# A GNN layer and a 64-expert FFN on one core: shared products deferred, a weight slot loaded earlier, another shape for the overflow turn

## The reference

```
x = x + relu(segment_sum(w * (layernorm(x) @ W)[dst], by src) + bias)      # 16384 edges
xt = layernorm(x);  scores = sigmoid(xt @ Wg.T + bg);  top 2 of 64, weights normed
nx = layernorm(xt)
y = sum over the 2 experts e of  weight * (silu(nx' @ W1[e] + b1) * (nx' @ W3[e] + b3)) @ W2[e] + b2
z = (silu(nxs @ Ws1 + bs1) * (nxs @ Ws3 + bs3)) @ Ws2 + bs2                 # shared expert, hidden 32
x = x + y + z
```

## Time and profile before

| | us |
|---|---|
| median of 3 runs | 459.57 |
| the profiled execution, its own time | 458.82 |
| its span, first to last instruction | 457.1 |
| TensorE busy | 391.7 (86%) |
| VectorE busy | 207.7 (45%) |
| ScalarE busy | 166.1 (36%) |
| GpSimd busy | 154.9 (34%) |
| mean granted TensorE clock | 0.932 of full speed |

### The profile page before, as it was taken

The page is one execution under the profiler, slowest core; times in us unless marked ns, Lnnn a source line. Parts: engine busy times, 40 slices in busy tenths (PEclk is TensorE's granted clock), DMA queues, the critical chain, the costliest instruction groups (busy, mean ns, idle before and its releaser), DMA issues.

```text
span 457.1 us, 6545 instructions
## 1 busy us (share of the span) xinstructions
PE 391.7 (86%) x1811; PEld 202.3 (44%) x1812; DVE 207.7 (45%) x685; ACT 166.1 (36%) x414; POOL 154.9 (34%) x262
## 2 busy tenths in 40 slices
PE   2699999999999987999999999986988979888600
PEld 1586767656565553344344443433434433343100
DVE  5889888216666586532333233313113123222036
ACT  9859999223223220233233323331213231131200
POOL 2575553014654657232333223323113122110000
PEclk9989999999999995899999999999889898898855
DMA  4999600100004545499999999999999999996068
GB/s 113 328 383 408 276 0 0 42 25 24 24 25 122 222 156 197 144 389 408 404 408 407 405 408 409 407 406 408 407 406 409 406 405 404 403 405 271 20 250 303
DMA packets 41779, 126.11 MB, mean 276 GB/s; under 512 B 7953, under 2 KB 8529, under 8 KB 41618
## 3 DMA queue, kind: packets, MB, share of 16 engines
q1 hardware_dynamic: 35954, 117.29, 66.3%
q0 software_dynamic: 5792, 8.43, 5.3%
HBM read 121.22 MB, written 13.39 MB: 294 GB/s over the span
## 4 chain that ended last, share of the span: by engine, by line
PE 81%; issue 5%; DMA 5%; DVE 3%; SPq 3%; POOL 1%; ACT 1%; ACTq 0%; DVEq 0%; POOLq 0%
PE bank L1295 29%; PE bank L1312 13%; PE bank L1168 12%; PE bank L1129 6%; PE bank L1136 6%; PE bank L1304 5%; PE bank L1288 4%; DMA w<-totals 2%; DMA X<-in_x_dram 2%; PE bank L1156 2%; PE bank L1187 1%; PE bank L1236 1%; PE bank L1177 1%; PE bank L1117 1%; SPq L398 1%
## 5 line engine op out<-in xcount | busy, mean ns | idle before, releaser
L1031 DVE SCALAR_TENSOR_TENSOR osl<-bank,b13T,osl 128x64 f32<-128x64 f32 x132 | 28.4, 277 | 171.5 <-ACT osl L675 171.5
L1295 PE MATMUL bank<-w,xhT 128*64 128x512 f32 x368 | 91.9, 645 | 14.7 <-issue 14.5
L668 ACT COPY xh<-bank 128x512 f32<-128x512 f32 x33 | 19.3, 585 | 149.0 <-PE bank L1295 149.0
L1168 PE MATMUL bank<-HW,AT 128*128 128x512 f32 x128 | 58.2, 592 | 0.0
L1295 PEld LDWEIGHTS bank<-w,xhT 128*64 128x64 f32 x368 | 28.6, 147 | 61.5 <-issue 60.1
L545 POOL DMA_INDIRECT totals<-osl,A x17 | 17.0, 1000 | 91.5 <-PE bank L1288 72.1
L1312 PE MATMUL bank<-w,osl 128*64 128x512 f32 x184 | 45.0, 608 | 3.2 <-DVE osl L1031 3.2
L545 POOL DMA_INDIRECT totals<-GW,A x16 | 16.0, 999 | 87.2 <-PE bank L1288 71.6
L587 ACT ACTIVATE osl<-iota,eT 128x128 f32<-128x128 f32 x128 | 39.0, 389 | 6.1 <-PE bank L1129 6.1
L541 POOL DMA_INDIRECT A<-nx_rows,A x33 | 34.4, 1041 | 10.5 <-issue 10.5
L1168 PEld LDWEIGHTS bank<-HW,AT 128*128 128x128 f32 x128 | 22.9, 191 | 21.0 <-issue 21.0
(11 more groups left out here) (208 smaller groups left out, 543.2 us busy)
## 6 DMA issues: line engine op xcount, KB each, us to landing
w<-in_L_ffn_W_dram SPq DMA_DIRECT2D x66, 1024.0 KB
A<-in_L_ffn_W_dram SPq DMA_DIRECT2D x15, 1024.0 KB
HW<-in_L_ffn_W_dram SPq DMA_DIRECT2D x10, 1024.0 KB
AT<-in_L_ffn_W_dram SPq DMA_DIRECT2D x5, 1024.0 KB
w<-totals SPq DMA_DIRECT2D x8, 512.0 KB, 7.5
w<-in_L_ffn_W_dram SPq DMA_DIRECT2D x6, 512.0 KB
X<-in_x_dram SPq DMA_DIRECT2D x4, 512.0 KB, 7.2
out_dram<-X SPq DMA_DIRECT2D x8, 256.0 KB, 5.7
```

Of the source, the lines that this page charges most:

```text
L1031: ins = v.scalar_tensor_tensor(hT[b][:, m, CAP * h:CAP * h + CAP], bank[4][:, (HC + m) * P + CAP * h:(HC + m) * P + CAP * h + CAP], b13T[: ...
L1168: ins = t.matmul(bank[4 + s % 2][:, :], AT[:, s % 2, k, :], HW[:, k, :], start=(k == 0), stop=(k == NB - 1))
L1295: ins = t.matmul(bank[2 + b][CAP * h:CAP * h + CAP, :], xe[b][:, c, CAP * h:CAP * h + CAP], up_w[v][:, h, :, c, :], start=(c == 0), stop=( ...
```

## The change

1. The list is read into the tile `xg[3]` instead of `M`, so its read does not wait for the last block of X. On SP the loads of slot 5 now stand at s = 6, ahead of the list's read and of the last `nx_rows` store.
2. `shared(5..7)` are taken out of the stretch before turn 0 and put into turns 20, 22 and 24 (`late_turn`), with their `add_shared`. `add_shared(0..2)` come before the overflow count on VectorE, `add_shared(3..4)` in turn 0, the last `transpose_stack` in turn 2. GpSimd does `stacked(7)` after the first gather instead of before it.
3. `keep_busy(bank, n)`: n transposes of the identity into a bank that is not read: 24 before turn 0's rows, 8 before the overflow turn's `up`, 14 before its `down`.
4. An overflow turn takes one expert and up to 128 more tokens (`steps` at 64, 192, ...), with `over_up`, `over_down`, `over_silu` and `over_product` on 128 rows at once: half as many, twice as wide instructions, and half the weights. `LIST` is 2 N, so `slots` and the memset and store that fill it are twice as large. The number of overflow turns is now the number of such experts (chunks), not half of it.

```diff
-LIST = N
+LIST = 2 * N
...
-        Lflat = M[0:PAIRS, 0, 0:2, :].rearrange("j a n -> j (a n)")
+        Lflat = xg[XG - 1][0:PAIRS, 0:2 * CAP * REC]
...
+        LATE = 5
+        late_turn = [PAIRS - 12, PAIRS - 10, PAIRS - 8]
...
                 if s == NB - 2:
-                    for i in range(2):
-                        sp.wait_ge(rec_out[i], 32 * DRAM_BLOCKS // 2)
-                    sp.wait_ge(x1_ready, NB)
-                    sp.dma_start(L, lists[:, :, 0:CAP * REC]).then_inc(list_in, 16)
-                if s == NB - 1:
                     sp.wait_ge(out_ps, NB)
                     load_up(RING // 2 + 1, RING // 2 + 1)
                     load_down(RING // 2 + 1, RING // 2 + 1)
+                    for i in range(2):
+                        sp.wait_ge(rec_out[i], 32 * DRAM_BLOCKS // 2)
+                    sp.dma_start(L, lists[:, :, 0:CAP * REC]).then_inc(list_in, 16)
...
             for j in range(AHEAD):
                 gather(TOK[:, j:j + 1], j)
+                if j == 0:
+                    stacked(NB - 1)
...
-            shared(5)
-            shared(6)
-            transpose_stack(NB - 1)
-            shared(7)
+            def keep_busy(spare_bank, n):
+                for i in range(n):
+                    t.transpose(spare_bank[:, (i % DC) * P:(i % DC + 1) * P], ident[:, :], ident[:, :])
...
+            def over_up(b):
+                for c in range(DC):
+                    ins = t.matmul(bank[2 + b][:, :], xe[b][:, c, :], up_w[OS][:, 0, :, c, :], start=(c == 0), stop=(c == DC - 1))
+                ins.then_inc(h_ps, 1)
...
+            pe.wait_ge(vs_ready, NB)
+            keep_busy(bank[0], 24)
             pe.wait_ge(xg_in[0], 16)
             turn_rows(0, 0)
             pe.wait_ge(extra_ready, 1)
-            pe.wait_ge(z_added, NB)
+            pe.wait_ge(z_added, 3)
...
+                if j in late_turn:
+                    shared(LATE + late_turn.index(j))
                 pe.wait_ge(xe_ready, j + 1)
+                if j == 0:
+                    pe.wait_ge(stackT_ready, NB - 1)
+                if j == PAIRS:
+                    pe.wait_ge(z_added, NB)
+                    keep_busy(bank[5], 8)
...
+                if j < PAIRS:
+                    up(j % 2, j % SLOTS)
+                else:
+                    over_up(j % 2)
...
+            keep_busy(bank[5], 14)
             down_of(PAIRS)
```

More of the change, by code:

```diff
@@ L27 @@
 OVER = 2 * N // CAP
+STEPS = N // P
 REC = 2
@@ L525, in stacked @@
                 g.tensor_tensor(stack[i][:, 0:64], weighted, other, ALU.add).then_inc(stack_ready, 1)
-            for s in range(NB + 1):
-                if s < NB:
-                    deviations(s)
+            for s in range(NB):
+                deviations(s)
                 if s > DRAM_BLOCKS:
@@ L682, in result, with over_silu @@
                 a.copy(ysb[i], bank[6 + b][:, :]).then_inc(y_ready, 1)
[L684 to L686 removed]
+            def over_silu(j, b, t):
+                e = act.value_load(over_expert[0:1, ds(t, 1)], min_val=0, max_val=EXPERTS - 1)
+                act.wait_ge(hT_ps, j + 1)
+                for m in range(HC):
+                    ins = a.activation(sl[b][:, m, :], bank[4][:, m * P:m * P + P], ACT.Silu, bias=b13T[:, 0, m, ds(e, 1)])
+                ins.then_inc(sl_ready, 1)
             for j in range(PAIRS + 1):
@@ L971, in _ @@
             stack_out(NB - 2)
+            for b in range(3):
+                add_shared(b)
             dve.wait_ge(count_ps, 1)
-            mark(v.tensor_scalar(steps[:, 0:CHUNKS - 1], iota[0:64, 1:CHUNKS], float(CAP), None, ALU.mult))
+            mark(v.tensor_scalar(steps[:, 0:STEPS], iota[0:64, 0:STEPS], float(P), float(CAP), ALU.mult, ALU.add))
             mark(v.tensor_scalar(expert_at, spare[0:64, :], float(CHUNKS), 1.0 - EXPERTS * CHUNKS - N * CHUNKS, ALU.mult, ALU.add))
             link(v.tensor_copy(count, list_bank[0:64, 128:129]))
[L976 to L981, removed]
+            link(v.tensor_scalar(passed[:, 0:STEPS], steps[:, 0:STEPS], count, None, ALU.is_lt))
+            v.tensor_reduce(extra, passed[:, 0:STEPS], AX, ALU.add).then_inc(extra_ready, 1)
             def over_table():
@@ L1035, in product, with over_product @@
                 ins.then_inc(hT_ready, 1)
+            def over_product(j, b, e):
+                dve.wait_ge(sl_ready, j + 1)
+                for m in range(HC):
+                    ins = v.scalar_tensor_tensor(hT[b][:, m, :], bank[4][:, (HC + m) * P:(HC + m) * P + P], b13T[:, 1, m, ds(e, 1)], sl[b][:, m, :],
+                                                 ALU.add, ALU.mult)
+                ins.then_inc(hT_ready, 1)
             def over_at_expert(t):
-                return [dve.value_load(over_expert[0:1, ds(2 * t + h, 1)], min_val=0, max_val=EXPERTS - 1) for h in range(2)]
+                return dve.value_load(over_expert[0:1, ds(t, 1)], min_val=0, max_val=EXPERTS - 1)
             rows(0, 0)
@@ L1049, in _ @@
                     rows(j + 1, (j + 1) % 2)
+                if j == 0:
+                    for b in range(3, LATE):
+                        add_shared(b)
+                    dve.wait_ge(stack_ready, NB)
+                if j == 2:
+                    stack_out(NB - 1, bank[5])
+                if j in late_turn:
+                    add_shared(LATE + late_turn.index(j))
                 if j == PAIRS // 2:
@@ L1297, in up, with over_down @@
                 ins.then_inc(h_ps, 1)
+            def over_up(b):
+                for c in range(DC):
+                    ins = t.matmul(bank[2 + b][:, :], xe[b][:, c, :], up_w[OS][:, 0, :, c, :], start=(c == 0), stop=(c == DC - 1))
+                ins.then_inc(h_ps, 1)
+            def over_down(j, b):
+                pe.wait_ge(hT_ready, j + 1)
+                for m in range(HC):
+                    ins = t.matmul(bank[6 + b][:, :], hT[b][:, m, :], down_w[OS][:, 0, m, :], start=(m == 0), stop=(m == HC - 1))
+                ins.then_inc(y_ps, 1)
             def turn_hidden(j, b):
```

110 lines of the change are left out of this document (59 added, 51 removed).

## The result

The changed kernel takes 455.86 us (median of 7 runs, 454.87 to 457.12); the kernel before, run beside it, 459.0 us (7 runs, 457.39 to 460.67). The ratio is 0.9934, with a 95% interval of 0.9911 to 0.9958: faster by 3.1 us, where 7.5 us were forecast. A second measurement of the same two kernels (label a2_change_again) gave 455.83 against 458.38, ratio 0.9942 [0.9916, 0.9968]. The profiled execution took 455.27 us; its span is 453.5 us (before: 457.1), its mean granted clock 0.959 (before: 0.932).

A forecast was written before the change was run, and what follows sets the result against it. Weight stream bounds it from about 300 us, starting when `up(0)` ends. Gain 7.5 us: 2.0 start, 1.1 wait, 1.8 clock in `up(32)`, about 1.1 silu and product, 1.5 clock in `down(32)`; forecast 452.1 us, range 449.0 to 457.0.

The forecast's parts named there:

- the start term: Start of the weight stream: `up(0)` ends 2.0 us earlier, between a loss of 1 and a gain of 5.
- the list lands near 170.7: List's read behind slot 5's weights on SP: lands near 170.7 us, where it landed at 166.3 before.
- 4 us, if its record scatters are slowed too: Upper bound on how late `list_ready` comes, before turn 0; the lower bound was nothing, if the list passes the weights.
- `list_ready` at 174.9: Before the first gather: `rank(7)` 1.9 us late at about 172.5, so `list_ready` at 174.9 instead of 172.75.
- The end term: Last turn: 1.1 us wait, 1.8 clock in `up(32)`, about 1.1 silu and product, 1.5 clock in `down(32)`.
- the plateau from the 17th slice on: Weight stream in the profile before: DMA share 9 tenths, 403 to 409 GB/s from about 188 us.
- Hidden parts: Late shared products in turns 20, 22, 24 and the doubled `slots` fill cost nothing; uncovered, 0.9 us each and 1.3 us.
- A: Rival: identity transposes before turn 0 and in the last turn do not hold the clock; gain 2.6, 457.0 us; 15%.
- B: Rival: the list before turn 0 isn't held up by the weights; start gain 4 to 5, 449.5 us; 12%.
- C: Rival: list, gathers and `stacked(7)` chain is longer; `up(0)` unmoved, gain 5.5, 454.1 us; with loss of 1, 455.1; 10%.
- D: Rival: the overflow loop runs a second turn because two experts exceed 64 tokens; about 21 us more, 473 us; 3%.

The follow-up runs named there:

- e4: Changed kernel with slot 5's loads issued after the record scatters landed, still ahead of the list's read: 457.51 us, ratio 0.9957 to the kernel before.
- e1: Changed kernel with slot 5's loads back behind the list's read and last row store: 450.43 us, ratio 0.9815 to the kernel before.
- e7: Changed kernel without the three deferred shared products in turns 20, 22 and 24 and their additions: 455.72 us, ratio 0.9941 to the kernel before.
- e5: Changed kernel with the overflow turn's weight loads doubled to 3.15 MB again, second half not read: 456.39 us, ratio 0.9945 to the kernel before.
- e3: Changed kernel without its 46 identity transposes: 457.92 us, ratio 0.9976 to the kernel before.
- e2: e1 with `stacked(7)` on GpSimd moved behind the second gather: 450.79 us, ratio 0.981 to the kernel before.
- e11: e2 without the 8 and the 14 identity transposes, the 24 kept: 448.48 us, ratio 0.9765 to the kernel before.
- e9: e1 without the 8 identity transposes before the overflow turn's `up`: 449.35 us, ratio 0.9808 to the kernel before.
- e10: e1 without the 8 and the 14 identity transposes, the 24 kept: 448.42 us, ratio 0.9774 to the kernel before.
- e8: e2 with 14 instead of 24 transposes at the start and ScalarE's overflow register load moved earlier: 450.12 us, ratio 0.9817 to the kernel before.

## Why the prediction was wrong

**The step that failed** is the start term, "I take 2.0 us; ends: a loss of 1 (everything late) and a gain of 5". It measured a loss of 1.6 us in the first profile and of 0.1 in the second, or of 1.1 and 0.8 counted from the record scatter. The mechanism was the one named (the list is held up by the weights); its size was wrong.

The numbers are those of the first profile.

- "Traffic begins some 1.6 us after an issue ... the list lands near 170.7": it landed at 173.45, 2.75 us later. Two things were missed. The read waits for the record scatters, and these took 7.33 us beside the weights, against 2.11 in e4, where nothing stood beside them. The prediction set "4 us, if its record scatters are slowed too" as a bound and did not weigh that the loads had been moved past exactly this wait. And the load itself ran slower at its start than the 410 GB/s that was used, so that e4's list, with the scatters out of the way, landed at 174.42 all the same. Two windows of the changed kernel (columns as above; the last is GB/s, the load's traffic begins at about 162):

```profile
160.50:164.00 3.50, 3.50 (x16) 1.95 (x14) 2.95 (x8) 0.09 (x1) 2.02 (x5) 1.00 0.61 102
164.00:168.00 4.00, 3.18 (x17) 1.87 (x16) 3.00 (x20) 1.79 (x4) 3.36 (x10) 1.00 0.89 357
```

- "`list_ready` at 174.9": it was 179.12. Of the 4.2 us, 2.75 are the list and 1.45 are TensorE, which the late list left idle for 4.92 us and then at half clock: `shared(4)` (L1251) took 2.01 us where 1.1 was used. The timeline of the changed kernel:

```profile
160.91 0.90 SPq L320 DMA_DIRECT2D HW<-in_L_ffn_W_dram  x2
...
168.78 0.66 SPq L348 DMA_DIRECT2D A<-slots  x1
...
173.50 0.44 PE L1232 MATMUL bank<-ident,A 32*128 32x32 f32 x2 [4.92 <-DMA A<-slots]
...
179.55 5.12 PE L1299 MATMUL bank<-ident 128*128 128x128 f32 x24
```

- From there the prediction held. First gather to second 3.1 us (3.1 forecast), second gather to `up(0)` 3.6 us (3.6), the 24 transposes 5.12 us (5.1 at half clock) and free, `up(0)` 3.61 (3.65 at full clock, 4.3 in the mean that was taken). In e1, where the list is on time, `up(0)` ends at 184.79, a gain of 4.0 within the stated ends, and the kernel takes 450.43 us. The 7.5 us of the prediction would have been too few without this one order.

**The end term** was forecast at 5.5 us and measured 4.5 (4.0 in a2). The wait before the last `up` is gone and 0.87 us of transposes stand there (0.9 forecast); the last `up` takes 3.44 (3.44); `down(31)` takes 1.89 and the last `down` 1.97, where 1.72 was taken for both; from the end of the last `up` to the end of the last `down` it is 6.59 us (8.82 before, 6.15 forecast). The other part is the stream, 0.7 us longer between `up(0)` and `up(31)` than before, and this is its first 12 us: 309 GB/s instead of 331, which is 0.65 us at 407 GB/s. The prediction had the plateau from the 17th slice on; the earlier trace rows have 144 GB/s in the 17th and 389 in the 18th, so the head of the stream was never at full rate.

**Hidden parts.** The deferred products cost nothing (e7), the doubled table nothing that e1's list shows, the bytes no more than their wait (e5), as predicted.

**The rivals.** A is refuted (e3, and the clock's windows above). Its sum was a little low, too: 14 transposes at half clock are 3.0 us and end at 427.7, not 427. B, an undelayed list, did not happen, but e1 makes it so and comes at 450.43; the prediction had 449.5 for it. C named a gain of 5.5 with a loss of up to 1 at the start for another reason, the gathers; its 455.1 is nearest to the time by luck, for the gathers were not at fault. D did not happen: there is one overflow turn, and the rows are gathered 33 times, as forecast.

**What stays open.** Why the load of slot 5 starts slowly; what holds down the first 12 us of the stream when `up(0)` ends early (e2 280 GB/s, e11 290); and when the clock falls in a pause as short as those of e9 and e10.

The best version measured is e11 (or e10, which can't be told from it): the change, with slot 5 behind the list and without the 8 and 14 transposes, 2.35% faster than the kernel before, against the change's 0.66%. The intervals of e1, e2, e8 and e9 overlap with theirs, so only the order on SP is shown to be worth it.

## What to carry to other kernels

When bulk loads move ahead of a small transfer, price every small transfer that is then in flight or queued, on every queue, and what waits for it: here scatters on another queue paid 4 to 5 us and a read on the same one 2.5 to 3 us (8 us where it alone paid), for 3.15 MB that no turn before the sixth uses. Find first what starts the stream that bounds the kernel, and let nothing stand ahead of that. A latency chain that comes late also leaves its engine idle, and then the engine's own work on the chain runs at half clock: add this to the delay (here 1.45 on 2.75 us).

## What the runs showed of the hardware that was not expected

- The last two scatters of 128 small records, issued as a 3.15 MB load began on another queue, landed 6.3 to 7.45 us after the second was issued (six profiles), and 2.11 us after it without the load (e4).
- A 32 KB read queued right behind 3.15 MB landed after 10.04 us, one issued some 7 us after the loads still after 4.6 to 5.3 us, and one with nothing ahead after 2.2 us.
- While twenty-four identity transposes ran in a row, the granted clock rose from 0.50 to 1.00; with 14, in one execution, it was at 0.50 behind them. After the 24 it fell back to 0.50 where TensorE then stood idle for 1.34 and 1.10 us (e9, e10), and did not where it stood idle for 0.94 us (e1).
- The stream of weights ran at 280 to 338 GB/s in its first 12 us and at 406 to 407 behind them.
- Eight records of float32 matmuls of 128 rows against 512 columns took 3.44 us, 16 records of 64 rows 3.65 us, both at full clock: joining the rows saved only 0.2 us.
